# Multiplying the kept tiles of the second pass two at a time, and building the late tiles first

## The reference

```
h  = relu(layernorm(x))
x  = x + gcn2(gcn1(h))                 # gcn: y[dst] += norm * (h @ W)[src], over all edges and loops
h  = relu(layernorm(x))
W  = (silu(edge_attr @ mlp_w1 + b1) @ mlp_w2 + b2) * cutoff(edge_weight)
agg = segment_mean((h @ lin1_w)[src] * W, dst)
x  = x + silu(agg @ lin2_w + lin2_b) @ lin_w + lin_b
```

## Time and profile before

| | us |
|---|---|
| three timed runs | 1470.44, 1467.88, 1466.33 |
| median | 1467.88 |
| profiled execution, span from its first to its last instruction | 1784.9 |

### The profile page before, as it was taken

The page is one execution under the profiler, slowest core; times in us unless marked ns, Lnnn a source line. Parts: engine busy times, 40 slices in busy tenths (PEclk is TensorE's granted clock), DMA queues, the critical chain, the costliest instruction groups (busy, mean ns, idle before and its releaser), DMA issues.

```text
span 1784.9 us, 36572 instructions
## 1 busy us (share of the span) xinstructions
PE 1367.6 (77%) x12469; PEld 1149.4 (64%) x12470; DVE 920.1 (52%) x3249; ACT 577.9 (32%) x1265; POOL 1013.1 (57%) x1039
## 2 busy tenths in 40 slices
PE   3345888778778877777588888888887678878787
PEld 1234776667666766666478878778876356556565
DVE  4954555565556655664435455445444334444444
ACT  3745554444445444544003312303210111111111
POOL 7575564554555555555555565665665456555563
PEclk9956998999999998998689999999998668877887
DMA  3244455555555555556646757757755424323422
GB/s 110 80 119 127 148 160 141 157 158 165 158 154 170 157 151 157 148 159 189 196 124 196 224 144 203 213 157 211 215 141 156 114 50 98 86 77 85 95 73 58
DMA packets 260338, 255.28 MB, mean 143 GB/s; under 512 B 136211, under 2 KB 217800, under 8 KB 259253
## 3 DMA queue, kind: packets, MB, share of 16 engines
q1 hardware_dynamic: 217269, 165.00, 32.3%
q0 software_dynamic: 42880, 87.88, 18.8%
HBM read 182.45 MB, written 70.31 MB: 142 GB/s over the span
## 4 chain that ended last, share of the span: by engine, by line
PE 51%; another core or an unknown queue 18%; DVE 9%; issue 9%; ACT 8%; ACTq 3%; DMA 1%; SPq 1%; DVEq 1%
PE ps_product L2118 18%; PE ps_banks L2074 10%; PE ps_pack L2092 7%; ACT adjacency L1207 5%; PE ps_banks L2162 3%; PE ps_banks L2056 2%; PE ps_pack L2255 2%; PE ps_banks L2274 1%; ACTq L1237 1%; PE ps_banks L2263 1%; ACT packed_T L1243 1%; PE ps_product L2255 1%; DMA src_raw<-in_src_dram 1%; PE ps_banks L2154 1%
## 5 line engine op out<-in xcount | busy, mean ns | idle before, releaser
L2118 PE MATMUL ps_product<-adjacency,table_parts 128*128 128x232 bf16 x4704 | 552.3, 270 | 14.8 <-issue 9.8
L1057 POOL DMA_INDIRECT ring_parts<-node_table_parts,src_idx x384 | 377.4, 983 | 317.2 <-PE ps_banks L2056 183.3
L1057 POOL DMA_INDIRECT ring_parts<-node_table,src_idx x384 | 379.1, 987 | 256.7 <-issue 108.7
L1207 ACT CAST adjacency<-ps_banks 128x550 f32 x504 | 336.6, 668 | 486.7 <-PE ps_banks L2074 234.9
L2118 PEld LDWEIGHTS ps_product<-adjacency,table_parts 128*128 128x128 bf16 x4704 | 469.6, 101 | 37.3 <-issue 14.6
L2074 PE MATMUL ps_banks<-code_onehot,lo_onehot 128*128 128x400 bf16 (+2 forms) x1494 | 243.8, 274 | 98.2 <-ACT adjacency L1207 68.2
L1057 POOL DMA_INDIRECT ring_parts<-node_table,packed_src x216 | 204.4, 946 | 159.0 <-issue 66.7
L2092 PE MATMUL ps_pack<-pack_onehot,edge_in 128*67 128x96 f32 x1664 | 198.2, 264 | 82.3 <-ACT packed_T L1243 45.7
L2074 PEld LDWEIGHTS ps_banks<-code_onehot,lo_onehot 128*128 128x128 bf16 x1494 | 151.1, 117 | 159.4 <-issue 90.0
L1598 DVE TENSOR_SCALAR code_onehot<-code_iota,code_T 128x600 bf16<-128x600 bf16 x504 | 179.5, 383 | 133.9 <-PE ps_banks L2074 89.8
L2092 PEld LDWEIGHTS ps_pack<-pack_onehot,edge_in 128*67 128x67 f32 x1664 | 165.0, 151 | 98.5 <-issue 95.3
(11 more groups left out here) (282 smaller groups left out, 1427.6 us busy)
## 6 DMA issues: line engine op xcount, KB each, us to landing
kept_tiles<-adjacency SPq DMA_DIRECT2D x98, 406.0 KB
adjacency<-kept_tiles SPq DMA_DIRECT2D x98, 406.0 KB
edge_in<-in_edge_attr_dram SPq DMA_DIRECT2D x207, 128.0 KB
packed_attr<-packed_T SPq DMA_DIRECT2D x8, 864.0 KB
adjacency<-packed_attr SPq DMA_DIRECT2D x6, 1152.0 KB
ring_parts<-node_table,src_idx POOLq DMA_INDIRECT x384
ring_parts<-node_table_parts,src_idx POOLq DMA_INDIRECT x384
node_table_parts<-table_parts SPq DMA_DIRECT2D x7, 672.0 KB
```

The lines of the kernel that those rows point to most:

```text
L1057: gps.indirect_dma_start(to, None, rows, bass.IndirectOffsetOnAxis(index, 0)).then_inc(gathered[s], 16)
L1207: nc.scalar.copy(adjacency[:, b, :, bass.ds(at, n)], count_columns(m, 0, n).rearrange("p n b -> p b n")).then_inc(chunk_copied, 1)
L2118: product = mm(ps_product[:, 0:COLS], table_parts[:, k, part, :], adjacency[:, buffer_of(c, tile), k, :], start=(k == 0 and part == 0), st ...
```

## The change

LATE_TILES becomes (0, 1, 2, 3), so pass 1 now gathers the groups of these tiles and builds, multiplies and stores tiles 4 to 17. In pass 2 the four late tiles come first, one at a time, 6 slots each; the three that are built in the pass are built in the first 5 of the 6 slots of the tile ahead. Then come the 14 kept tiles as 7 pairs, each over 7 or 8 slots: one matmul reads both halves of `adjacency` and writes 464 columns of `ps_product`, and DVE adds its two halves to `acc` one after the other. Parts are loaded for both tiles of a pair as the same part of the pair ahead is used. Node updates now come at most one a slot instead of one in 1.5 slots.

```diff
-LATE_TILES = (0, 5, 10, 15)
+LATE_TILES = (0, 1, 2, 3)
+LATE_SLOTS = 6
-BUILD_SLOTS = 12
+BUILD_SLOTS = 5
...
     def second_pass():
-        plan = Pass(gather_groups(range(TILES)), list(range(TILES)))
+        pairs = [tuple(KEPT[i:i + 2]) for i in range(0, len(KEPT), 2)]
+        plan = Pass(gather_groups(range(TILES)), [(tile,) for tile in LATE_TILES] + pairs)
         slots = len(plan.groups)
-        at = [FIRST_PRODUCT + (slots - REST_SLOTS) * order // TILES for order in range(TILES + 1)]
...
+        late = LATE_SLOTS * LATE_COUNT
+        at = [LATE_SLOTS * i for i in range(LATE_COUNT)]
+        at += [late + (slots - REST_SLOTS - late) * i // len(pairs) for i in range(len(pairs) + 1)]
...
+        for i in range(LATE_COUNT - 1):
+            number = len(KEPT) + 1 + i
+            plan.clears[at[i]] = number
+            place_build(plan, number, at[i], BUILD_SLOTS)
+        for i in range(PARTS):
+            plan.loads.setdefault(at[LATE_COUNT - 1], []).append((LATE_COUNT, 0, i))
+            plan.loads.setdefault(at[LATE_COUNT - 1] + 1 + LATE_SLOTS * i // PARTS, []).append((LATE_COUNT, 1, i))
+        for order in range(LATE_COUNT + 1, len(plan.tiles)):
+            for i in range(PARTS):
+                slot = at[order - 1] + 1 + (at[order] - at[order - 1]) * i // PARTS
+                plan.loads.setdefault(slot, []).extend([(order, 0, i), (order, 1, i)])
-        update_slots(plan, last_group, add_slots, 1.5, slots - 2)
+        update_slots(plan, last_group, add_slots, 1, slots - 2)
...
             def load_tile(order, b, i):
+                if order > LATE_COUNT:
+                    sp.wait_ge(part_used[2], PARTS * (order - 1) + i + 1)
+                elif b == buffer_of(2, LATE_TILES[-1]):
+                    sp.wait_ge(part_used[2], PARTS * (LATE_COUNT - 1) + i + 1)
                 else:
-                    sp.wait_ge(seventh_loaded[i], table_loaded(i))
+                    sp.wait_ge(part_used[2], PARTS * (LATE_COUNT - 1))
...
                         load_x(2, 0)
-                        for i in range(PARTS):
-                            load_tile(LOADED[0], i)
...
             def add_tile(c, order):
+                for i, tile in enumerate(PLAN[c].tiles[order]):
...
+                    acc_done(vec.tensor_tensor(to, to, ps_product[:, i * COLS:(i + 1) * COLS], ALU.add),
+                             tile_added[c], tiles_before(c, order) + i + 1)
...
                 for part in range(3):
-                    product = mm(ps_product[:, 0:COLS], table_parts[:, k, part, :],
-                                 adjacency[:, buffer_of(c, tile), k, :],
+                    product = mm(ps_product[:, 0:len(tiles) * COLS].rearrange("p (t n) -> p t n", n=COLS),
+                                 table_parts[:, k, part, :], adjacency[:, first:first + len(tiles), k, :],
```

More of the change, by code:

```diff
@@ L162, in first_pass @@
     def first_pass():
-        plan = Pass(gather_groups(KEPT), KEPT)
+        plan = Pass(gather_groups(KEPT), [(tile,) for tile in KEPT])
         slots = len(plan.groups)
@@ L187, in second_pass @@
+        at += [late + (slots - REST_SLOTS - late) * i // len(pairs) for i in range(len(pairs) + 1)]
+        for order in range(len(plan.tiles)):
             place_product(plan, order, at[order], at[order + 1] - at[order])
-            number = BUILT.index(tile)
-            if tile in LATE_TILES and number + 1 < TILES:
-                plan.clears[at[order + 1] + 1] = number + 1
-                place_build(plan, number + 1, at[order + 1] + 1, BUILD_SLOTS)
-        before = None
-        for order, tile in enumerate(plan.tiles):
-            if tile not in LATE_TILES:
-                if before is not None:
-                    for i in range(PARTS):
-                        slot = at[before] + 1 + (at[before + 1] - at[before]) * i // PARTS
-                        plan.loads.setdefault(slot, []).append((order, i))
-                before = order
@@ L200, in second_pass @@
-        add_slots = {plan.tiles[order]: s for s, order in plan.adds.items()}
-        update_slots(plan, last_group, add_slots, 1.5, slots - 2)
+        for i in range(LATE_COUNT - 1):
[5 more added lines that the diff above has]
+            plan.loads.setdefault(at[LATE_COUNT - 1] + 1 + LATE_SLOTS * i // PARTS, []).append((LATE_COUNT, 1, i))
@@ L202, in second_pass @@
+        for order in range(LATE_COUNT + 1, len(plan.tiles)):
+            for i in range(PARTS):
+                slot = at[order - 1] + 1 + (at[order] - at[order - 1]) * i // PARTS
+                plan.loads.setdefault(slot, []).extend([(order, 0, i), (order, 1, i)])
+        add_slots = {tile: s for s, order in plan.adds.items() for tile in plan.tiles[order]}
+        update_slots(plan, last_group, add_slots, 1, slots - 2)
         return plan
@@ L239, in gnn_kernel, with tiles_before @@
     place_packs()
-    LOADED = [order for order, tile in enumerate(PLAN[2].tiles) if tile not in LATE_TILES]
+    def tiles_before(c, order):
+        return sum(len(tiles) for tiles in PLAN[c].tiles[:order])
     LAST_PACK_SLOT = max(PLAN[2].packs)
     def buffer_of(c, tile):
-        number = BUILT.index(tile)
-        if c == 1:
-            return number % 2
-        return len(KEPT) % 2 if tile in LATE_TILES else 1 - len(KEPT) % 2
+        if c == 2 and tile in KEPT:
+            return KEPT.index(tile) % 2
+        return BUILT.index(tile) % 2
     def packed_edge(tile):
@@ L1601, in clear @@
             def clear(number):
[L1603 to L1605 removed]
+                b = number % 2
+                if number > len(KEPT) + 1:
+                    dve.wait_ge(part_used[2], PARTS * (number - len(KEPT) - 1))
                 elif number >= 2:
@@ L2104, in multiply @@
             def multiply(c, order, k):
-                tile = PLAN[c].tiles[order]
+                tiles = PLAN[c].tiles[order]
+                late = c == 2 and order < LATE_COUNT
                 if k == 0:
-                    wait(pe, tile_added[c], order)
-                    if c == 1 or tile in LATE_TILES:
-                        pe.wait_ge(chunk_copied, TILE_CHUNKS * (BUILT.index(tile) + 1))
+                    wait(pe, tile_added[c], tiles_before(c, order))
+                    if c == 1 or late:
+                        pe.wait_ge(chunk_copied, TILE_CHUNKS * (BUILT.index(tiles[0]) + 1))
                 if order == 0 and k % BP == 0:
```

33 lines of the change are left out of this document (13 added, 20 removed).

## The result

| | runs | median us | lowest, highest |
|---|---|---|---|
| before | 4 | 1468.04 | 1466.33, 1470.44 |
| changed | 4 | 1487.78 | 1485.44, 1489.21 |

The changed kernel takes 1.0131 of the time of before, with a 95% interval of 1.0107 to 1.0155: 19.7 us, 16 to 23. The forecast was 1468.4 with a range of 1450 to 1486. Repeated in another comparison, the ratio was 1.0138 (1.0114 to 1.0161).

What follows compares the result with a forecast made beforehand. PE was taken to bound pass 2, with POOL's gathers only 0.23 us a slot behind. Terms -2.5 - 9 + 12 - 3 - 1 + 0 + 4 = +0.5 us on 1467.88 gave 1468.4, range 1450 to 1486.

Steps and rivals of the forecast that it cites:

- The stops without a cause: PE in pass 2: 2058 fewer instructions at 5.3 ns of unexplained stops each, 10.9 us, taken as 9 us saved.
- The start of pass 2: Seven tile loads no longer precede the edge attributes on SP: 3 us saved; the burst moves to slot 18.
- Builds: 84 chunks of pass 2 built in 5 slots instead of 12: more PE waits at pass 1's rate, 12 us lost.
- Rival C: The chunk chain paces pass 2's first 18 slots; builds cost 26 us instead of 12, total 1482; chance 0.24.
- Wide matmuls: Pass 2's pairs: 1029 fewer matmuls, each pair costing 195.8 ns against 198.2 for two single ones, 2.5 us saved.
- Boundaries: Tile boundaries in pass 2 fall from 18 to 11: 2 us less PE waiting, 1 us for second adds, sum -1.
- Loads of pairs: Tile loads for pairs, concentrated in slots 18 to 66 of pass 2, cost 0 us, bounds 0 and 18.
- Rival D: Loads of pairs arrive late in slots 25 to 66 of pass 2: 17 us lost, total 1485; chance 0.08.
- The end: Four node blocks instead of two remain after pass 2's last slot, delaying pass 3's first gather: 4 us lost.
- The limit by the gathers: POOL's gathers in pass 2, at 6.28 us a slot, let the kernel gain at most 18 us.
- Pass 1: Pass 1 keeps the same slots, builds, products and packs, only other groups: 0 us, within 2 either way.

Runs made afterwards that it cites:

- the clean profile: The kernel before, unchanged, profiled once more because its first profile was 317 us longer than the timed runs; span 1464.7 us.
- e2_early_loads: The changed kernel, with the first pair's first tile loaded part by part over slots 13 to 18, not in one burst; 1.0136 of before.
- e7_zero: The changed kernel, with ACT's long copy that clears packed_T in pass 2 issued one slot earlier, in slot 12; 1.0093 of before.
- e1_singles: The changed kernel, with nearly all blocks of a pair multiplied by two matmuls of 232 columns instead of one of 464; 1.0162 of before.
- e4_tail: The kernel before, with four node blocks instead of two left after pass 2's last slot; 1.0050 of before.
- e11_two_parts: The kernel before, with one third of pass 2's product (the third bf16 part of the table) left out; 0.9934 of before.
- e9_all: The changed kernel with four edits: early part-by-part tile loads, evenly spread chunks, ACT's clearing copy in slot 12, last pair's tiles multiplied singly; 1.0082 of before.

## Why the prediction was wrong, step by step

- **The stops without a cause (-9): this step failed.** They were taken from an execution 317 us longer than the timed ones, and the clean profile has none (0 instead of 47.7 us). The forecast named that time as "a candidate for what shrank there", priced it all the same at 9 of its 11 us, and so hid a loss of that size.
- **The start of pass 2, "two slots, which the attributes outlast": failed for what it left out.** The burst was moved to slot 18, the attributes did outlast it, and the x block, named in the same sentence as one slot ahead, did not. 4.5 us of wait, 0.5 behind it and 2.7 for the low clock; `e2_early_loads` shows the burst to be the cause. No term stood for it. The -3 itself was near: the pack's wait in slot 0 fell from 2.1 to 0.7 us, and 1.1 less were lost to the low clock there, which ended 4.7 us after the window sum instead of 8.5. How much of this second part is the change's is not settled, as the other changed kernels had it end after 5.0 to 7.2 us.
- **Builds (+12): right in size, by luck.** Waits for ACT and DVE at counts and products 7.0 us, short waits and work at counts and packs 3.8, low clock 1.7: 12.5. But it is not pass 1's rate for each chunk. The 0.17 us came from the slower execution too; the clean profile has 0.05 in pass 1, which would have given 4 us for 84 chunks, and the changed kernel has 0.08. What filled the term is one copy of ACT that the denser slots no longer cover (3.8 us with the low clock, by `e7_zero`) and waits too short to be listed. Rival C is out at 0.08 us a chunk; its threshold of 0.21 should, by its own sum, be 0.18.
- **Wide matmuls (-2.5): right**, 2.6 us by the two profiles and 2.8 by `e1_singles`. The row that the forecast went by, 232 and 256 columns, held at 464. The Trainium skill's two points for a real kernel's stream ("TensorE: Matmul & The Clock Gate", section "Back-to-back issue gap") gave 125 ns, and the trace has 195.8. The prediction says of these two points that they lie below the page's formula for single matmuls; of the gap that the section gives, this is so at 512 columns (131 against 216 ns) and not at 128 (81 against 56).
- **Boundaries (-1): 0.** There were no waits of PE for the adds left to save.
- **Loads of pairs (0): right.** PE waited for no tile load from slot 24 on, with the DMA engines busy for 0.87 of it and 258 GB/s. Rival D is out.
- **The end (+4): right**, 5.3 us by `e4_tail`. The 2.6 us a block are partly luck: 1.13 us and four stages of half that, as the prediction has it, make 3.4. In the changed kernel the end shows as 1.8, since POOL had got 3.3 us further ahead of PE by slot 74 (its last gather for that slot was done 12.1 us ahead of PE's window sum, against 8.8).
- **The limit by the gathers (18 us): too high.** It is 8 us by the clean profile and `e11_two_parts` confirms it. The 6.28 us a slot that it went by held a stop of 1.47 us; the clean profile has 5.1.
- **Pass 1 (0): nothing speaks against it.** Slot 0's window sum starts at 742.1 to 748.3 us in the five profiles with the order of before and at 742.0 to 748.1 in the eight with the new one.

Measured, the sum is -2.6 + 0 + 12.5 - 1.4 + 0 + 7.9 + 1.8 = 18.2, against 18.2 in the stage. That it comes out to the tenth is chance: the 1.1 us less at the low clock in slot 0 and some 1.5 more in window sums, products and nodes are left out, and nearly cancel. The two steps that failed account for the miss: without the -9 the forecast would have been +9.5, and with the 7.9 us of the x block +17.4.

## What to carry to other kernels

Hold a profile's span against the timed runs before using any of its rows as a price, and give no term to time that the timed runs do not have. When a burst of transfers is moved, list every later transfer in the same queue with its lead, and price the shortest lead, not the longest. Before packing work for an engine that is busy everywhere, find the second-busiest engine's own pace: it caps what the change can win, while what it can lose has no such cap.

## What the runs showed of the hardware

- The price of a stop of PE can be more than its length. In the six profiles with the stop of 1.6 to 2.2 us behind ACT's long copy, 3.4 us at the lower clock (1.2 instead of 2.4 GHz) followed, 1 to 13 us after its end; in the two in which that copy was moved, none. With the stops of 2.8 to 4.9 us for the x block came 3.4 to 6.8 us of it, each time from at most 1.1 us ahead of the stop's end to 2.0 behind it. It is no rule for single stops: one of 2.4 us in `e2_early_loads` and in `e9_all` had none behind it, and `e1_singles` had 3.4 us of it with no stop near.
- A load of 64 KB (an x block) issued behind 3.7 MB of tile loads took 9.6 us to land, 8.4 to 10.1 in six profiles; without the burst one took 3.9 (`e9_all`).
- ACT's read of a slot's chunk columns into registers is no fixed cost: some 0.3 us at the least, 0.75 and 1.33 in turn with six chunks a slot, also beside tile loads, 2.1 to 2.2 beside a store of 864 KB, and 3.74 and 4.42 beside that store and tile loads. It shows only as idle time of ACT with no cause.
- POOL's gathers of 128 rows have a pace of their own: 0.95 us and 0.3 between two, and 421.4 us for the 328 of pass 2 with PE far ahead (`e11_two_parts`).
